# A Mamba, mLSTM and attention-graph layer on one core: a PSUM bank of its own for three projections, units of the scan ordered part by part, first transfers reordered

## Time and profile before

| | |
|---|---|
| median of 3 runs | 1310.47 us |
| the profiled execution | 1308.01 us, of which the span from first to last instruction is 1306.2 us |
| PE busy | 1098.0 us (84%), weight loads beside it 822.0 us |
| DVE busy | 1053.6 us (81%) |
| ACT busy | 720.6 us (55%) |
| POOL busy | 2.9 us, SP only issues |
| DMA queue | 17.9% of 16 engines, 76 MB |
| granted TensorE clock, mean | 0.939 |
| start of F(0), F(1), ..., F(7) (copy L799) | 239.4, 376.5, 513.6, 651.4, 788.7, 925.8, 1063.2, 1190.3 us |

### The profile page before, as it was taken

One profiled execution on the slowest core, in us unless ns is written; L12 is line 12 of the kernel. 1 busy time (PEld: TensorE's weight loads), 2 busy tenths in 40 slices (PEclk: granted clock), 3 DMA queues, 4 the chain that ended last, 5 costly groups with the idle time before them and its releaser, 6 DMA issues. The chain is left out here.

```text
span 1306.2 us, 27811 instructions
## 1 busy us (share of the span) xinstructions
PE 1098.0 (84%) x11504; PEld 822.0 (63%) x11504; DVE 1053.6 (81%) x1683; ACT 720.6 (55%) x1692; POOL 2.9 (0%) x10
## 2 busy tenths in 40 slices
PE   3845668988999899989988998899888988897886
PEld 2723445766676667666666666666666666676665
DVE  2289887799999999999999999999999889725112
ACT  1434532576657665776567556755576646444332
POOL 0000000000000000000000000000000000000000
PEclk9767775999999999999999999999999989999998
DMA  6440343004100410030112211030104000000000
GB/s 190 122 178 32 107 153 113 33 3 130 41 26 33 132 42 25 34 105 28 50 49 62 71 50 49 16 117 33 58 3 130 33 25 34 2 1 10 2 1 9
DMA packets 53710, 76.14 MB, mean 58 GB/s; under 512 B 15376, under 2 KB 38672, under 8 KB 53456
## 3 DMA queue, kind: packets, MB, share of 16 engines
q1 hardware_dynamic: 53584, 74.37, 17.9%
HBM read 63.60 MB, written 10.75 MB: 57 GB/s over the span
## 5 line engine op out<-in xcount | busy, mean ns | idle before, releaser
L979 DVE TENSOR_TENSOR_SCAN unit_buf<-dec,unit_buf 128x512 f32<-128x512 f32 x256 | 311.9, 1218 | 11.7 <-ACT dec L753 11.0
L753 ACT ACTIVATE dec<-dts,a_neg 128x254 f32<-128x254 f32 x512 | 225.6, 499 | 42.5 <-DVE unit_buf L979 37.3
L972 DVE TENSOR_TENSOR unit_buf<-dtus,bs 128x512 f32<-128x512 f32 x256 | 175.0, 686 | 6.3 <-DMA dtus<-dt_rows 2.5
L990 DVE TENSOR_TENSOR unit_buf<-unit_buf,cs 128x512 f32<-128x512 f32 x256 | 175.3, 685 | 0.5
L1087 DVE TENSOR_REDUCE mx<-heads 128x16 f32<-128x2048 f32 x48 | 109.2, 2276 | 50.1 <-PE heads L602 50.0
L487 PE MATMUL ps<-unit_buf,fold 128*32 128x256 f32 x1024 | 89.0, 420 | 52.4 <-DVE unit_buf L990 52.3
L825 ACT ACTIVATE pr<-heads 128x512 f32<-128x512 f32 x192 | 99.1, 603 | 49.0 <-PE heads L617 49.0
L571 PE MATMUL ps<-node,wq_f 128*128 128x256 f32 x384 | 93.6, 387 | 7.8 <-ACT node L840 7.8
L640 PE MATMUL heads<-node,we_f 128*128 128x256 f32 x384 | 94.7, 389 | 0.0
L647 PE MATMUL heads<-aT,wo_f 128*128 128x256 f32 x384 | 93.7, 387 | 0.9 <-DVE aT L1096 0.9
L581 PE MATMUL heads<-wv_f,node 128*128 128x256 f32 x384 | 91.8, 382 | 0.0
(11 more groups left out here) (178 smaller groups left out, 1777.8 us busy)
## 6 DMA issues: line engine op xcount, KB each, us to landing
dts<-dt_rows SPq DMA_DIRECT2D x32, 512.0 KB, 3.8
dtus<-dt_rows SPq DMA_DIRECT2D x32, 512.0 KB, 5.2
node<-in_w_edgeT SPq DMA_DIRECT2D x18, 256.0 KB, 3.6
dt_rows<-dt SPq DMA_DIRECT2D x32, 128.0 KB, 2.4
dt_rows<-th SPq DMA_DIRECT2D x32, 128.0 KB, 2.5
bs<-bc_rows SPq DMA_DIRECT2D x32, 128.0 KB, 4.6
cs<-bc_rows SPq DMA_DIRECT2D x32, 128.0 KB, 4.3
xin<-in_x SPq DMA_DIRECT2D x8, 256.0 KB, 6.2
```

The source lines that it names most:

```text
L753: last = fn(dec[k % 2][:, a, :, 1:L], dts[c % 2][:, blk, :].rearrange("p (b t) -> p b t", b=GB)[:, :, 1:L], ACT.Exp, scale=a_neg[:, c, blk ...
L972: v.tensor_tensor(inf[k % 2][:], dtus[c % 2][:, 2 * pair:2 * pair + 2, :], bs[:, q:q + 1, :].broadcast_to([P, 2, T]), ALU.mult).then_inc(s ...
L979: v.tensor_tensor_scan(hst[k % 2][:].rearrange("p a b -> p (a b)"), dec[k % 2][:].rearrange("p a b t -> p (a b t)"), inf[k % 2][:].rearran ...
L990: v.tensor_tensor(prd[(i * UNITS + k) % PRDS][:], hst[k % 2][:], cs[:, q:q + 1, :].broadcast_to([P, 2, T]), ALU.mult).then_inc(sig["outflo ...
```

## The change

- `MB` is renamed `ED` and holds the keys of nodes 1 to 5, `edge` and `node`. The mLSTM moves to `MA` for the groups from 1 on (`ML = (ED, MA)`), where it takes turns with A; for group 0 it keeps the old bank.
- In F, `edge` moves from behind the four `attend` to a place between `score` and `attend`, and for nodes 2 to 5 `v` moves from behind the preceding `node` to a place ahead of it. `score` no longer waits for the key copy; `edge` does.
- A unit's decays, feed, weigh and scan become four steps with slots of their own; work and sizes stay. `U_AT` has 156 entries where it had 61, and all slot lists are new, with a shift for each group (`A_SH`, `U_SH`, `X_SH`).
- The transfers of `a_neg` go to POOL's queue, and its exponential and negation to ACT, ahead of the first decay. The input weights come in two halves, those of node 0 ahead of the output projection's.
- For group 0 the first chunk goes from SBUF to SBUF (`first_chunk`), beside the store to DRAM, and `spread` is issued in A step 9. The first three steps of P stand ahead of A(0) step 7 instead of around it, and the next three ahead of U(0).
- Keys and values of the gates have the same input, so their two halves of the gate matrix are added once (`gate_sum`): four matmuls at L516 instead of six.

```diff
-    F_STEPS += [("f", "node", _c)]
+    F_STEPS += [("f", "score", _c), ("f", "edge", _c), *(("f", "attend", _c * STEPS + s) for s in range(STEPS))]
     if 2 <= _c + 1 < NODES:
         F_STEPS += [("f", "v", _c + 1)]
+    F_STEPS += [("f", "node", _c)]
 F_STEPS += [("f", "out", 0)]
 FSLOTS = len(F_STEPS)

...
-for _k in range(UNITS + 1):
-    U_STEPS += [("u", "unit", _k)] if _k < UNITS else [("u", "last", 0)]
+U_STEPS += [("u", "feed", 0)]
+for _k in range(UNITS):
+    U_STEPS += [("u", "dec", _k)]
+    if _k + 1 < UNITS:
+        U_STEPS += [("u", "feed", _k + 1)]
+    if _k >= 1:
+        U_STEPS += [("u", "weigh", _k - 1)]
+    U_STEPS += [("u", "scan", _k)]
     if _k % CUNITS == 1 and CUNITS < _k < (IC - 1) * CUNITS:
...
 for _h in range(XH):
...

-A_AT = [-90, -86, -76, -69, -62, -58, -57, -52, -44, -43, -42]
...
+U_AT = [-38, -38, -38, -36, -35, -34, -34, -33, -32, -31, -31, -30, -30, -30, -30, -30, -30, -29, -29, -26, -26,
+        -24, -24, -24, -24, -24, -24, -21, -21, -21, -21, -21, -20, -19, -19, -18, -18, -18, -18, -18, -18, -17,
...
+U_SH = [-1, 1, 1, 1, 1, 1, 1, 1]
+X_SH = [0, 0, 0, 0, 0, 0, 0, 0]
+AT = (("a", A_STEPS, A_AT, A_SH), ("u", U_STEPS, U_AT, U_SH), ("x", X_STEPS, X_AT, X_SH))

 ORDER = [(FSLOTS * g + n, 0, g, n, step) for g in range(NG) for n, step in enumerate(F_STEPS)]
-for _rank, (_name, _steps, _at) in enumerate(AT):
-    ORDER += [(FSLOTS * (g - 1) + at, 1 + _rank, g, n, step)
+for _rank, (_name, _steps, _at, _shift) in enumerate(AT):
+    ORDER += [(FSLOTS * (g - 1) + at + _shift[g], 1 + _rank, g, n, step)
               for g in range(NG) for n, (step, at) in enumerate(zip(_steps, _at))]
 ORDER += [(at, 4, 0, n, step) for n, (step, at) in enumerate(zip(P_STEPS, P_AT))]
 ORDER = [(step, g) for _, _, g, _, step in sorted(ORDER)]
...
-        MA, MB, MY, FA = [es.enter_context(nc.psum_tensor(f"ps{j}", [P, 512], F32)) for j in range(4)]
+        MA, ED, MY, FA = [es.enter_context(nc.psum_tensor(f"ps{j}", [P, 512], F32)) for j in range(4)]
...
+        ML = (ED, MA)
+        K_BANK = (X2, *(ED[:],) * (NODES - 1))
...
+            def first_chunk(dst, src, name):
+                for k in range(BLKS):
+                    sp.dma_start(dst[0][:, k, :], src[k * SD:(k + 1) * SD, 0, :].unsqueeze(1).broadcast_to([SD, SN, T])
+                                 ).then_inc(sig[f"{name}_first"], 16)
...
+                    if i == 0:
+                        for q in range(NGRP):
+                            spread_rows(0, q)
...
+                    if i == 0:
+                        first_chunk(dts, dt, "dt")
...
+                    if i == 0:
+                        first_chunk(dtus, dtu, "dtu")
...
+                if i:
+                    spread_rows(i, q)
+
+            def spread_rows(i, q):
...
+                if i == 0 and c == 0:
+                    return
...
-            for c in range(IC):
-                for k in range(BLKS):
-                    load(a_neg[:, c, k, :], vecs[k * SD:(k + 1) * SD, V_ALOG + c * NS:V_ALOG + (c + 1) * NS].rearrange(
-                        "d (n g) -> d n g", n=SN), "alog_loaded")
-            load(win[:], w_in, "win_loaded")
-            load(wx[:], w_x, "const_loaded")
-            load(wdt[:], w_dt, "const_loaded")
-            load(rowv[:], rowvecs.partition_broadcast(P), "const_loaded")
+            load(win[:, :, 0:I], w_in[:, :, 0:I], "win_loaded")
+            load(win[:, :, I:2 * I], w_in[:, :, I:2 * I], "wing_loaded")
+            load(wx[:], w_x, "wx_loaded")
+            load(wdt[:], w_dt, "wx_loaded")
+            load_weights(0)
             load(wout[:], w_out, "const_loaded")
             load(wgate[:], w_gate, "const_loaded")
...
+            load(rowv[:], rowvecs.partition_broadcast(P), "const_loaded")
...
+                    if i <= 2:
+                        after(pe, "dt_read", i - 1, 2)
+                    else:
+                        after(pe, "n0T_ready", i - 2, 1)
...
+                    if i == 0 and j % 2 == 0:
+                        pe.wait_ge(sig["wing_loaded" if j else "win_loaded"], 16)
...
-                    after(pe, "n0T_ready", i - 1, 1)
+                    if 1 <= i < NG - 1:
+                        after(pe, "dt_read", i + 1, 2)
+                    elif i == NG - 1:
+                        after(pe, "n0T_ready", i - 1, 1)
...
+                    if i == 0:
+                        pe.wait_ge(sig["const_loaded"], 16 * 3)
...
-                    for k in range(3 * HC):
+                    if i == 0:
+                        pe.wait_ge(sig["gate_sum"], 1)
+                    for k in range(2 * HC):
...
+                    after(pe, "node_ready", i - 1, NODES * HC)
+                else:
+                    after(pe, "node_ready", i, (c - 1) * HC)
...
                 after(pe, "smax_read", i, c + 1)
-                if c + 1 < NODES:
-                    after(pe, "k_read", i, c + 2)
                 tr(FA[:, 0:P], mx[:], ident).then_inc(sig["maxT_ps"], 1)
...
+                if c + 1 < NODES:
+                    after(pe, "k_read", i, c + 2)
+                else:
+                    after(pe, "node_ready", i, c * HC)
...
-                        mm(X1[:, a * T:(a + 1) * T], we_f[c][:, k, a * P:(a + 1) * P], src[:, k, :],
+                        mm(ED[:, a * T:(a + 1) * T], we_f[c][:, k, a * P:(a + 1) * P], src[:, k, :],
...
+                    act.wait_ge(sig["alog_loaded"], 16 * IC * BLKS)
+                    fn(a_neg[:], a_neg[:], ACT.Exp).then_inc(sig["setup_act"], 1)
+                    act.wait_ge(sig["setup_act"], 1)
+                    fn(a_neg[:], a_neg[:], ACT.Copy, scale=-1.0).then_inc(sig["setup_act"], 1)
+                    act.wait_ge(sig["setup_act"], 2)
...
+                        act.wait_ge(sig["dt_first"], 16 * BLKS)
+                    after(act, f"dt_in{c % 2}", i, 16 * (c // 2 + c % 2))
...
-                    fn(node[SLOT[c]][:, a, :], X1[:, a * T:(a + 1) * T], ACT.Identity,
+                    fn(node[SLOT[c]][:, a, :], ED[:, a * T:(a + 1) * T], ACT.Identity,
...
-            act.wait_ge(sig["alog_loaded"], 16 * IC * BLKS)
-            fn(a_neg[:], a_neg[:], ACT.Exp).then_inc(sig["setup_act"], 1)
...
-                v.tensor_scalar(negsel_bf[:], strip[:], -1.0, None, ALU.mult)
-                dve.wait_ge(sig["setup_act"], 1)
-                v.tensor_scalar(a_neg[:], a_neg[:], -1.0, None, ALU.mult).then_inc(sig["vec_consts"], 1)
+                v.tensor_scalar(negsel_bf[:], strip[:], -1.0, None, ALU.mult).then_inc(sig["vec_consts"], 1)
...
-            def unit(i, k):
-                if k == 0:
-                    feed(i, 0)
-                if k + 1 < UNITS:
-                    feed(i, k + 1)
-                if k >= 1:
-                    weigh(i, k - 1)
-                scan(i, k)
-
-            def unit_last(i, _):
-                weigh(i, UNITS - 1)
...
+                    if i == 0:
+                        dve.wait_ge(sig["const_loaded"], 16 * 3)
+                        v.tensor_tensor(wgate[:, HC:2 * HC, :], wgate[:, HC:2 * HC, :], wgate[:, 2 * HC:3 * HC, :],
+                                        ALU.add).then_inc(sig["gate_sum"], 1)
...
+            for c in range(IC):
+                for k in range(BLKS):
+                    pool.dma_start(a_neg[:, c, k, :], vecs[k * SD:(k + 1) * SD, V_ALOG + c * NS:V_ALOG + (c + 1) * NS
```

90 lines of the change are left out of this document (48 added, 42 removed), and 5 rows, old and new, of the table U_AT.

## The result

The change makes the kernel slower: a median of 1317.65 us in six runs (1307.94 to 1319.09) against 1309.93 us for the kernel before in six runs of the same job, a ratio of 1.0047 with a 95% interval of 1.0025 to 1.0069. The forecast was 1274.5 us with a range from 1254 to 1294. The profiled execution took 1318.01 us, its span is 1316.2 us, and its mean granted clock 0.917 where it was 0.939. PE is busy for 1121.5 us, 23.5 more than before, though it has less to do.

The account below looks back on a forecast made before the run. The prediction took PE's chain of matmuls and waits to set the repeating stretches, with DVE's limit near 133 us. Its terms summed to -36 us, -13 of it in six stretches, giving 1274.5 us, range 1254 to 1294.

Parts of the forecast that it names:

- (b): Repeating stretch: `edge` ahead of `attend` covers PE's wait for the exponentials, 1.4 us gained in each.
- (d): Repeating stretch: without `v` between `node` and the next `q`, PE waits for the node copy, +1.1 us.
- (a): Repeating stretch: the transposed maxima no longer wait for the key copy, 1.0 us gained in each.
- (c): Repeating stretch: two of the four context gate matmuls go, 0.9 us gained in each.
- R1: Rival: stretches don't shrink, as DVE's place in the list sets their length; 1287.5 us, chance 0.16.
- First transfers: Start: `a_neg` on POOL's queue lets input weights issue sooner, -10.0 us; POOL's transfers taken at 0.65 each, hidden.
- P around A(0): Ahead of F(0): L407 moved before `x_proj` delays it by 2.6 us but frees 1.0 behind it, net +1.6.
- U(0) and X(0): Ahead of F(0): U(0) -1.5 us by finer order; X(0) -4 by moved input projections and fewer gate matmuls.
- (f): Repeating stretch: bank `MA` is handed over twice between A and X; taken as 0 us.
- R3: Rival: the shared bank makes X's first step wait for ACT's second `dt` read; 1320 us at 5.5, chance 0.07.
- R2: Rival: finer parts also remove the reduction wait, stretches fall to DVE's limit of 133 us; 1261 us, chance 0.13.
- R4: Rival: at the start, late `a_neg` or node 0 weights shrink the -10 to -4; 1280 us, chance 0.05.

Follow-up runs that it names:

- e5: The changed kernel with, on TensorE alone, `edge` of nodes 0 and 5 put back behind the fourth `attend`: 1303.03 us, ratio 0.9959.
- e4: The changed kernel plus eight idle bf16 matmuls at four places per group where PE pauses: 1295.26 us, ratio 0.9913.
- e9: The kernel before with two of four convolution taps left out (VectorE's work): 1310.1 us, ratio 1.0002.
- e10: The kernel before with a third of the gate matmuls, half of `x_proj` and half of the Mamba output projection (TensorE): 1304.07 us, ratio 0.9946.
- e14: The kernel before with half the input of the attention output projection at nodes 1, 3 and 5 (TensorE): 1310.75 us, ratio 1.0018.
- e13: The kernel before with the multiplication with C halved in every second scan unit (VectorE): 1301.34 us, ratio 0.9935.
- e7: The changed kernel with TensorE's `edge` of all six nodes behind the fourth `attend`, and the banks of before: 1360.08 us, ratio 1.0379.

## Why the prediction was wrong

**Its first error is a cost that it did not list.** It priced every wait by its length and none by what it does to the clock, whose term in the stretches was nothing. Step (b) put `edge` ahead of `attend` and booked -1.4. It never asked what the place behind `attend` would be without it; step (d) looked at the gap behind `node` alone, and no step at what the new slots leave PE at X's heads and its end. The waits for the division came to 19.4 us where 0.9 were (6.2 of them by `edge`'s place, as e5 has 13.2), at X's end to 11.2 where 0.6 were, at the heads to 5.1 at L578. PE's waits are 1.5 us longer in all, but they lie otherwise, and the clock falls: about 57 us at the lower level for 8. e4 and e5 show that this carries the loss, as filling pauses takes 22 and 14.6 us off by medians (18 and 12 by ratios), and stretches at full clock take 137.2 us again. The table of the clock was looked at ahead of F(0) (0.72) and not in the stretches, where 1.00 stood and could only fall. The Trainium skill (TensorE: Matmul & The Clock Gate, section "A second HAM failure mode: psum-queue depth-cycling") tells of a kernel whose TensorE pauses briefly but often between groups of matmuls, and whose clock goes back and forth between its two levels. This trace agrees, with pauses of 0.6 to 2.0 us in an engine that is busy for 90% of the stretch.

**Its second error is the inference on which the sum of the stretches rested**: "five microseconds less of DVE's work bought nothing, and the length comes from PE's chain". The first half was right and e9 repeats it. The second doesn't follow: e10 and e14 take 3.8 and 2.2 us from PE, and that buys at most 0.3. The trace of the kernel before had a row that spoke against it, the stretch of F(5), with 23 of PE's instructions fewer and no shorter for it, though at a slightly lower clock:

```profile
925.80:1063.20 137.40, 122.28 (x1375) 91.23 (x1373) 127.72 (x198) 85.93 (x203) 0.00 (x0) 0.98 0.17 53
```

Work that is missing in one place tells whether that place is on the chain, no more. Hence (a) to (c), booked at -3.3 us, are worth nothing: at full clock a stretch with all of them takes 137.2 (e4). R1 gave the right outcome for the stretches at full clock; its reason, VectorE's place in the list, isn't shown, as e9 took 3 us from VectorE for nothing and e13 3.6 for 1.2. Its 1287.5 is 8 us under e4, whose stretches are still short of the clock in two places. The test that the text gave for its own failure, that "PE's waits merely change their names", is what came: the kernel before has 13.0 us without a matmul in its second stretch (137.10 - 124.13), e5 13.0 (137.26 - 124.22).

**Point by point.** First transfers: -10.0 forecast, -8.5 measured at PE's first matmul, as the layer norm was late next. The price of POOL's queue: 0.55 us for each transfer where 0.65 was taken, hidden. Of the Trainium skill's warning there (DMA: Bandwidth & Descriptors, section "SWDGE vs HWDGE vs iDMA") nothing shows: all 16 were issued by 12.1, and nobody waited for them. It was no hard test, as VectorE was busy for 3.0 us of the 8.8. P around A(0): +1.6 forecast, +1.9 measured (8.5 at PE's first matmul, 6.3 left at `x_proj`, 6.7 at the mean square behind it, L502 at 36.88 for 43.54). First chunk: -2.3 forecast; from the issue of the first `dt` transfer to the first feed are now 9.6 us for 10.9, -1.3. U(0) and X(0): -5.5 forecast, -2.6 measured (11.3 less 8.7). Together -11.3 where -16.2 was forecast. The two input projections that X(0) gave up were not free, as the forecast had it ("their number stays"): the six stretches hold 16 matmul instructions more, 3.9 us of PE, against the 5.6 that (c) took. F(7): -3.8, as forecast. F(6): +1.4 for -3, at a clock of 0.96 where it was 0.99. (f) and R3, the shared bank: at `MA`'s handover PE waits in the six stretches for 1.0 us in all, for the copy of X's node input (L467 for L860), as the text foresaw, and for nothing at X's first step; e7 leaves open whether the bank costs in another way. R2: not near. R4: it didn't come, the edit does at the start what it says.

By terms the forecast missed the span by 46 us: 4.9 ahead of F(0), 13 + 23.7 = 36.7 in the stretches, 4.4 in F(6).

## What to carry to other kernels

When a step is moved, look at the place that it leaves, and ask of each pause on TensorE whether a pause stood there before; moving eight matmuls back, or filling pauses with idle ones, was worth 12 to 22 us here, where the new order itself had gained 7.4 (3.6 ahead of F(0) and 3.8 in F(7)). Look for the short pauses too: those of 0.6 and 0.7 us between X's heads stood ahead of nearly half of the time at the lower clock. Don't conclude from busy times, nor from one piece of work that is missing, which engine sets a woven schedule: take some work from each in turn, ScalarE included, and only believe a length that answers. A list of slots tuned by hand holds for one order only, so pieces of such a change can't be tried one by one.

## What was unexpected of the hardware

That pauses so short cost so much. In the changed kernel PE runs without a break at 486.59, yet at half its speed, in the timeline of TensorE alone:

```profile
480.01 0.66 PE L588 MATMUL ps<-vaug,ml_buf 128*128 128x65 f32 x4 [0.64 <-DVE ml_buf L1096]
...
482.53 0.77 PE L578 MATMUL ps<-ml_buf,negid 4*128 4x256 f32 x2 [0.68 <-DVE hrow L1102]
...
486.59 3.58 PE L629 MATMUL heads<-wv_f,node 128*128 128x256 f32 x8
...
490.40 1.95 PE L697 MATMUL ps<-aT,wo_f 128*128 128x256 f32 x8
```

```profile
484.00:491.00 7.00, 7.00 (x51) 5.66 (x51) 4.04 (x7) 2.22 (x6) 0.00 (x0) 0.58 0.02 4
```

Eight matmuls take 3.58 us at 486.59 and eight alike 1.95 at 490.40. Between 484 and 491 the granted clock is 0.58 on average, while PE is busy for all 7.00 us; the pauses in the five microseconds before were 0.64 and 0.68. By e4's rows some eight microseconds at the lower level (0.97 over 140.91) cost a stretch 3.7 us, and this in a stretch in which PE was busy for over 90%. And the places of such falls differ from stretch to stretch under the same pauses. The spread of the runs goes with it: e4's six runs at 1293 to 1296 us have a mean granted clock of 0.939, its four at 1304 to 1307 one of 0.929 or 0.930, and of the changed kernel's runs the one at 1307.94 has 0.924, the other five, 1316.56 to 1319.09, have 0.914 to 0.917.
